# Clearing finished semaphores on SyncE while the experts run, and issuing eight query loads one stage later

## The reference, cut to what matters

```python
x = x + _L0_xattn_ref(ctx_1024, _layernorm(x), mask, ...)    # 16 heads of 16
x = x + _L0_attn_ref(_layernorm(x), ...)
x = x + _L0_ffn_ref(_layernorm(x), ...)                       # 12 experts, top 3 of 12, two layers
x = x + _L1_xattn_ref(_layernorm(x), ctx_1024, ctx_1024, ...) # 16 heads of 64
x = x + _L1_attn_ref(_layernorm(x), ...)
x = x + _L1_ffn_ref(_layernorm(x), ...)                       # quantised weights and activations
```

## Time and profile before

| | before |
|---|---|
| median of 3 runs | 1759.65 us |
| lowest, highest | 1758.5, 1762.81 us |
| the profiled execution itself | 1759.81 us |
| its span, first to last instruction | 1758.0 us |
| mean granted clock of TensorE | 0.943 |
| PE busy | 1562.5 us (89% of the span) |
| DVE busy | 1132.3 us (64%) |
| ACT, POOL busy | 875.0 us (50%), 685.5 us (39%) |

### The profile page before, as it was taken

The page is one execution under the profiler, slowest core; times in us unless marked ns, Lnnn a source line. Parts: engine busy times, 40 slices in busy tenths (PEclk is TensorE's granted clock), DMA queues, the critical chain, the costliest instruction groups (busy, mean ns, idle before and its releaser), DMA issues. The chain is left out here.

```text
span 1758.0 us, 42136 instructions
## 1 busy us (share of the span) xinstructions
PE 1562.5 (89%) x15980; PEld 882.6 (50%) x15980; DVE 1132.3 (64%) x1756; ACT 875.0 (50%) x1178; POOL 685.5 (39%) x535
## 2 busy tenths in 40 slices
PE   3999999999499999999777958999999999967772
PEld 1455455455133333333453426777777777753442
DVE  4665665665499999997337747666666666425356
ACT  2555555555167777778251014555555555523440
POOL 2431000000111111111053108999999999933500
PEclk9999999999689999999798969999999999988886
DMA  4787988888432222221300057565546555012000
GB/s 162 199 216 226 223 216 221 222 231 211 146 101 68 65 65 65 65 65 34 153 1 1 1 138 217 152 158 149 146 124 164 145 153 155 27 35 91 1 0 12
DMA packets 178076, 212.14 MB, mean 121 GB/s; under 512 B 57080, under 2 KB 151428, under 8 KB 173342
## 3 DMA queue, kind: packets, MB, share of 16 engines
q1 hardware_dynamic: 177376, 210.37, 43.3%
q10 hardware_dynamic: 576, 0.00, 0.0%
HBM read 122.71 MB, written 87.57 MB: 120 GB/s over the span
## 5 line engine op out<-in xcount | busy, mean ns | idle before, releaser
L1121 POOL TENSOR_TENSOR x_r<-x_p 128x1024 f16<-128x1024 f32 x256 | 479.0, 1893 | 24.0 <-ACT x_p L1097 16.9
L1136 DVE TENSOR_REDUCE x_mx<-a_all 128x2 f32<-128x1024 f32 x249 | 304.9, 1224 | 147.2 <-PE a_all L1020 147.2
L1097 ACT ACTIVATE x_p<-s_all 128x1024 f32<-128x1024 f32 x256 | 248.4, 1022 | 223.1 <-PE s_all L1003 223.1
L702 ACT ACTIVATE x_p<-s_all 128x1024 f32<-128x1024 f32 x256 | 261.0, 1023 | 49.2 <-PE s_all L612 41.9
L757 DVE TENSOR_REDUCE x_mx<-a_all 128x1 f32<-128x512 f32 x352 | 229.9, 684 | 16.7 <-PE o_all L623 8.7
L1003 PE MATMUL s_all<-x_q,x_k 64*128 64x256 f16 x3072 | 210.0, 269 | 0.0
L1038 PEld LDWEIGHTS o_all<-x_v,x_p 128*128 128x128 bf16 x2048 | 178.7, 97 | 40.1 <-issue 40.1
L1038 PE MATMUL o_all<-x_v,x_p 128*128 128x129 f16 x2048 | 197.3, 221 | 0.9 <-POOL x_r L1121 0.9
L1039 PE MATMUL o_all<-x_v,x_r 128*128 128x65 f16 x2048 | 192.5, 193 | 0.0
L1039 PEld LDWEIGHTS o_all<-x_v,x_r 128*128 128x128 f16 x2048 | 180.7, 98 | 0.0
L1003 PEld LDWEIGHTS s_all<-x_q,x_k 64*128 64x128 f16 x3072 | 149.4, 94 | 62.2 <-issue 0.8
(11 more groups left out here) (347 smaller groups left out, 2784.1 us busy)
## 6 DMA issues: line engine op xcount, KB each, us to landing
values<-vst SPq DMA_DIRECT2D x16, 2064.0 KB, 10.3
x_v<-values SPq DMA_DIRECT2D x32, 1032.0 KB, 5.2
keys<-kst SPq DMA_DIRECT2D x32, 1024.0 KB, 6.5
x_k<-keys SPq DMA_DIRECT2D x128, 256.0 KB, 5.1
x_k<-keys SPq DMA_DIRECT2D x192, 64.0 KB, 2.1
values<-vst SPq DMA_DIRECT2D x16, 528.0 KB, 11.5
x_v<-values SPq DMA_DIRECT2D x32, 264.0 KB, 2.6
cf<-in_ctxT SPq DMA_DIRECT2D x16, 512.0 KB, 9.5
```

Of the source, the lines that this page charges most:

```text
L702: act.activation(prob[g % NP][:], chip.s_ps[g % 2][:].rearrange("p (c q) -> p c q", q=SQ), ACT.Exp, scale=hd ** -0.5).then_inc(p_ready, 1)
L1097: act.activation(prob[g % NP][:], chip.s_ps[g % 2][:].rearrange("p (c q) -> p c q", q=SQ), ACT.Exp, scale=hd ** -0.5).then_inc(p_ready, 1)
L1121: pool.tensor_tensor(rest[g % NP][:], prob[g % NP][:], hi, ALU.subtract).then_inc(rest_done, 1)
L1136: dve.tensor_reduce(mx[a[1] % 2][:, n // 4, 2 * (n % 4):2 * (n % 4) + 2], chunk_banks(u, g)[:, :].rearrange("p (h c) -> p h c", h=2), AX.X ...
```

## The change: what it does

Two things are changed.

1. `recycle_semaphores` and its block are gone. `retire_semaphores`, called at the start of `experts`, sets aside the semaphores made so far; inside the experts' block SP, which had no work there, clears all of them one after the other; their numbers are given back after that block. Three semaphores of the expert weights that are still in use then are made with `lasting_sem`, outside the set. The 19 semaphores that `experts` makes for itself are not cleared and not handed out again.
2. In `project_queries_wide` the loads of the queries of units 2 and 3 (eight DMAs) are no longer issued; they are issued in `cross_attention_wide` instead, after the keys of unit 2 and ahead of the wait for the first `x_qm`.

```diff
-    def recycle_semaphores(self):
-        sems, self.sems = self.sems, []
-        with self.nc.Block() as block:
-            @block.gpsimd
-            def _(pool):
-                for s in sems[0::4]:
-                    pool.sem_clear(s)
...
-            @block.tensor
-            def _(pe):
-                for s in sems[3::4]:
-                    pe.sem_clear(s)
-        self.sem_scope.close()
+    def lasting_sem(self, name):
+        return self.ctx.enter_context(self.nc.semaphore(name))
+
+    def retire_semaphores(self):
+        old = self.sems, self.sem_scope
+        self.sems, self.sem_scope = [], self.ctx.enter_context(ExitStack())
+        return old
@@ project_queries_wide
                 buffers.load_keys(sp, 0, 1)
-                for u in range(2, 4):
-                    buffers.load_queries(sp, 0, u)
@@ cross_attention_wide
                 buffers.load_values(sp, 0, 0)
                 buffers.load_keys(sp, 0, 2)
+                for u in range(2, 4):
+                    buffers.load_queries(sp, 0, u)
                 sp.wait_ge(qm_turned, 32)
@@ ExpertWeights
-        self.router_loaded = chip.sem("ew_rld")
+        self.router_loaded = chip.lasting_sem("ew_rld")
...
-        self.loaded, self.split = chip.sem("ew_ld"), chip.sem("ew_split")
+        self.loaded, self.split = chip.lasting_sem("ew_ld"), chip.lasting_sem("ew_split")
@@ experts
+    old_sems, old_scope = chip.retire_semaphores()
...
         with nc.Block() as block:
+            @block.sync
+            def _(sp):
+                for s in old_sems:
+                    sp.sem_clear(s)
...
+    old_scope.close()
@@ perceiver
                 experts(chip, "moe", expert_weights)
-        chip.recycle_semaphores()
```

## The result

The changed kernel takes 1751.7 us (median of 4 runs, 1749.76 to 1753.48) against 1760.52 for the kernel before in the same comparison: ratio 0.9955, 95% interval 0.9941 to 0.9968. The ratio is not that of the two medians: it says 7.9 us less (5.6 to 10.4), where the medians lie 8.8 us apart. The forecast was 1751.3, 8.4 us less.

A forecast was written before the change was run, and what follows sets the result against it. Barriers set the time, by whichever engine comes last: TensorE's clears after the experts, SP's DMA issuing in the projection. 1759.81 - 4.4 - 4.0 = 1751.4 us, 1751.3 after a 0.16 us median correction; range 1749.0 to 1755.0.

The forecast's parts named there:

- Part 1: Between experts and ln3: clearing block and its barrier removed, 4.4 us gained; 121 clears on SP cost nothing.
- cover: In the experts' block: SP waits 76.0 us for their end, hiding its 121 clears, taken as 14.2 us.
- Part 2: At the projection's barrier: without eight loads the release moves from SP's end to DVE's, 4.0 us gained.
- The turn: Second cross attention, before first scores: the first small transfer still lands in 2.0 us, issued 0.6 us after traffic ends.
- The rival: Before the first scores: first turn lands in traffic, up to 3.6 us lost, total 1753 to 1755; chance 0.10.
- The clock: TensorE in layer norm and projection: stays at half speed despite shorter idle; nothing in the sum, +/- 1.5 us range.
- the 5.64 us row: Layer norm before the experts: after 5.64 us idle, eight transposes took the same 1.97 us, so half speed stays.

The follow-up runs named there:

- the twelvefold kernel: The changed kernel with every clear done 12 times on SP, 1452 clears instead of 121: 1764.29 us in one run.
- the loads alone: The kernel before with only the eight query loads moved behind the keys of unit 2, the clearing block kept: 1756.65 us, ratio 0.9985.
- The kernel with traffic: The changed kernel without SP's wait ahead of the values of unit 1, so 3 MB move around the first turn: 1760.33 us, ratio 1.0005.

## Why the prediction was right

- **Part 1, 4.4 us.** Right. Statistics of ln3 come 0.1 us after the experts' release instead of 4.5. The prediction did not split it: 4.1 for TensorE's clears, 0.3 for the barrier. SP's price was taken as 0.12 us a clear and is 0.06; it is under cover either way, and the twelvefold kernel shows where the cover ends.
- **Part 2, 4.0 us.** Right for the two together, 3.7 measured (22.3 to 18.6 us from release to release), since the low clock lasted 0.4 us longer in the projection (6.56 against 6.16). The end is DVE's drain, as forecast. But one sentence of the prediction failed: "Everything on SP in the layer norm and the projection starts 4.4 us earlier with its stage, so its relation to the arithmetic stays." SP's drain ends 3.4 us ahead of DVE's, not 1.2. Taking 35 clears off TensorE moved its instruction fetch out of the way of a store, and SP got through 1.9 us sooner for that alone. With the clears gone, the loads' move was worth 1.6 us in the profile, not 4.0; with the clears still there, 4.4. It didn't show in the sum because both ways the stage ends with DVE, as with the loads alone, where the store was still late. In this order the clears are worth 6.3 us in the profile and the loads 1.6, where the prediction had 4.4 and 4.0; that the sum came out all the same rests on DVE's place in the stage, which it had right.
- **The turn.** Landing 2.0 us, as forecast, with the engines quiet 0.4 us before it (forecast 0.6). By the Trainium skill ("DMA: Bandwidth & Descriptors", "Queues, rings and completion order") a completion lands only after all earlier writes of its engine. The kernel with traffic agrees in direction, 8.0 to 9.9 us, but there the packets are late too, so it does not show this rule by itself. Nor did it cost nothing, as the prediction drew from the engines' taking the queues in turn: with 3 MB about the turn the scores come 7.8 us later. The rival's price of up to 3.6 us came from the next turn's landing of 5.9 us, which was no upper bound.
- **The clock.** Half speed in spite of the shorter idle time, as forecast from the 5.64 us row. At the first scores it came back later, and the third group of scores starts 5.9 us after the first instead of 5.55.
- **The number.** Forecast and median lie 0.4 us apart, but the interval of the gain is 5.6 to 10.4 us: so close a hit is luck. What the profile bears out is each stretch, 4.5 us against 4.4 and 3.7 against 4.0.
- **In the profiled execution** the span fell by 6.3 us only, and the marks of the table say where: 0.8 us later already at the experts' release, which the change doesn't reach; then 4.5 and 3.6 us won; 0.3 lost from the projection's release to the scores, where ACT took 1.36 us to issue the turn instead of 1.20; 0.3 lost to the clock there; 0.3 after it. The medians fell by 8.8, and the ratio says 7.9. Two single profiles would have given the size wrongly by a quarter; the two stretches that the change reaches, 4.5 and 3.6, give 8.1 us.

## What to carry to other kernels

In a program of stages with a barrier each, list for every barrier which engine's drain is last: work on that engine before the barrier counts in full, and on any other nothing, until it becomes last. Housekeeping and issuing of DMAs go to the engine that idles, in the stage in which it idles, but keep bulk transfers away from a tiny transfer that everyone waits for. And where an idle stretch lets TensorE's clock fall just ahead of dense float32 work, a few matmuls that nobody reads are worth measuring.

## What was not expected of the hardware

- A fetch of TensorE's instructions (16 KB, 0.9 to 1.65 us on its DMA engine) can delay a 128 KB store, which then lands after 3.6 to 3.8 us instead of 1.7. Taking 35 clears off TensorE ended it, and between 37 and 38 clears at the experts' start one instruction made the difference.
- Clears follow each other every 0.06 us on SP, 0.07 on POOL and 0.12 on PE.
- A transfer of 2 x 0.5 KB lands in 2.0 us with quiet DMA engines and in 8.0 to 9.9 us amid 3 MB that SP issued from 2.1 us before it to 1.1 us after it and the stores that followed, though it went out on ACT's queue.
